# An AdaLN block with linear attention and top-2 experts: another order of the transfers on SyncE, and other orders on TensorE, VectorE and ScalarE

## The reference

```python
h = layernorm(x) * (1 + ca) + sa
x = x + ga * attn(h)          # 16 heads of 16; q, k = elu(.) + 1; causal linear attention:
                              # num = tril(q k^T) v + q S;  den = sum(q * cumsum(k));  out = num / den
h = layernorm(x) * (1 + cb) + sb
# experts: logits = h @ emb^T, top 2 of 8, softmax of the two, a token keeps a choice
# while its place among the expert's tokens (running count over all tokens) is <= 512
x = x + gb * sum_over_choices(weight * (relu(h @ W1[e]^T) @ W2[e]^T))
```

## Time and profile before

| what | us |
|---|---|
| median of three executions (lowest, highest) | 469.27 (468.74, 469.97) |
| the profiled execution, its own time | 468.47 |
| its span, first to last instruction | 466.7 |
| TensorE busy | 391.6 |
| VectorE busy | 334.7 |
| GpSimd busy | 225.4 |
| ScalarE busy | 204.7 |
| from the first scores of step 3 to those of the tail | 219.51 |

### The profile page before, as it was taken

How to read it: one execution, slowest core, us unless ns; L and a number is a source line. 1 busy time by engine, 2 the same in 40 slices (tenths; PEclk the granted TensorE clock), 3 DMA queues, 4 the chain that set the end, 5 groups by cost and what they waited for, 6 DMA issues and landing times.

```text
span 466.7 us, 9558 instructions
## 1 busy us (share of the span) xinstructions
PE 391.6 (84%) x3366; PEld 307.4 (66%) x3366; DVE 334.7 (72%) x876; ACT 204.7 (44%) x341; POOL 225.4 (48%) x231
## 2 busy tenths in 40 slices
PE   3696979999799899989989999896228999999981
PEld 0553748777577586767767778675107888888871
DVE  6573685999698698789879979867734656666640
ACT  1664335644545543554544572314105444444520
POOL 4223151553642480481473372442464788788454
PEclk9599899999899989989989999997558999999997
DMA  8102204006204404402510601546147688888343
GB/s 251 66 0 83 79 0 132 15 7 204 74 2 143 138 2 144 130 8 95 152 33 31 194 13 40 177 145 217 49 133 232 146 212 204 189 212 183 35 44 46
DMA packets 40340, 49.70 MB, mean 106 GB/s; under 512 B 5881, under 2 KB 32506, under 8 KB 40306
## 3 DMA queue, kind: packets, MB, share of 16 engines
q1 hardware_dynamic: 33138, 36.55, 24.8%
q0 software_dynamic: 7168, 12.72, 14.0%
HBM read 31.84 MB, written 17.42 MB: 106 GB/s over the span
## 4 chain that ended last, share of the span: by engine, by line
PE 39%; DVE 20%; issue 16%; POOL 8%; DMA 8%; ACT 4%; SPq 3%; POOLq 1%; DVEq 0%; ACTq 0%
DVE sT L1554 6%; PE bank L1345 4%; PE quad L1345 3%; PE bank L1347 3%; PE bank L1346 3%; PE quad L1347 3%; PE quad L1346 3%; PE quad L1085 3%; PE bank L1010 2%; PE bank L1117 2%; DMA rden_rows<-rden_flat 2%; DMA out<-x 2%; PE bank L1145 2%; DVE kcum L1520 2%; SPq L443 2%
## 5 line engine op out<-in xcount | busy, mean ns | idle before, releaser
L1554 DVE TENSOR_TENSOR sT<-quad,causal 128x1024 f32<-128x1024 f32 x64 | 74.6, 1206 | 1.6 <-PE quad L1085 1.6
L685 POOL DMA_INDIRECT out<-x,tok_i x32 | 52.6, 1643 | 25.2 <-DVE x L1859 18.5
L595 POOL TENSOR_TENSOR x<-x_sb,bo_g 128x1024 f32<-128x1024 f32 x8 | 18.9, 2363 | 76.2 <-DMA out<-x 76.0
L1085 PE MATMUL quad<-q_bd,kT 32*128 32x256 f32 x512 | 42.7, 403 | 6.9 <-DVE sT L1554 5.4
L1145 PE MATMUL bank<-wog,oT 128*128 128x256 f32 x128 | 36.2, 407 | 10.3 <-DVE oT L1544 10.3
L1345 PE MATMUL bank<-w_hi,in_hi 128*128 128x256 f32 x128 | 37.0, 289 | 6.2 <-DVE in_lo L1844 6.2
L674 POOL DMA_INDIRECT xg<-token_rows,tok_i x32 | 32.9, 1027 | 19.0 <-issue 9.1
L924 ACT ACTIVATE in_hi<-quad 128x512 fp32r<-128x512 f32 x32 | 19.1, 598 | 51.2 <-PE quad L1347 51.2
L1117 PE MATMUL bank<-sT,v_pad 128*32 128x128 f32 x1024 | 41.4, 281 | 0.0
L1844 DVE SCALAR_TENSOR_TENSOR in_lo<-quad,in_hi 128x512 fp32r<-128x512 f32 x32 | 22.1, 692 | 22.8 <-ACT in_hi L924 22.8
L1085 PEld LDWEIGHTS quad<-q_bd,kT 32*128 32x128 f32 x512 | 26.8, 184 | 15.3 <-DVE sT L1554 8.1
(11 more groups left out here) (219 smaller groups left out, 1016.9 us busy)
## 6 DMA issues: line engine op xcount, KB each, us to landing
token_rows<-h SPq DMA_DIRECT2D x8, 528.0 KB, 3.6
x_sb<-x SPq DMA_DIRECT2D x8, 512.0 KB, 3.7
token_rows<-mod_all SPq DMA_DIRECT2D x8, 512.0 KB, 4.8
out<-x SPq DMA_DIRECT2D x8, 512.0 KB, 5.1
w_sb<-w1T SPq DMA_DIRECT2D x8, 512.0 KB, 4.5
w_sb<-w2T SPq DMA_DIRECT2D x8, 512.0 KB, 4.7
rden<-rden_rows SPq DMA_DIRECT2D x56, 64.0 KB, 2.3
mod_all<-mod_rows SPq DMA_DIRECT2D x8, 384.0 KB, 4.1
```

The source lines that it names most:

```text
L685: gp.indirect_dma_start(out=out_rows, out_offset=bass.IndirectOffsetOnAxis(ap=tok_i[:, 1, at:at + 1], axis=0), in_=y_sb[q][:, t, :], in_of ...
L1085: last = mm(quad[:, r, k * 2 * P:(k + 1) * 2 * P].rearrange("p (s i) -> p s i", s=2), kT[b.p][at, k, tok(t)], q_bd[b.p][at, k, :, tok(t)], ...
L1554: v.tensor_tensor(sT[t % 2][:, 8 * a:8 * (a + 1), :].rearrange("p (r s) i -> p r (s i)", s=2), quad[:, 2 * a:2 * a + 2, :].rearrange("p r ...
```

## The change

- SyncE: in a full step the order becomes `rden_to_dram(attend)`, `load_ga(front)`, `load_x(early)`, `rden_to_heads(attend)`, `den_to_dram(front)`, `den_by_rows(front)`, `load_mod(attend)`, `x1_to_out(route)`, and then the wait for `row_on`, `rows_h` and `rows_gate`.
- GpSimd: `row_h(route)` goes from behind `norm2` to the end of the step, behind `norm1` and `q_times_kcum`.
- TensorE: `front_h` of half 0 comes first, before `scores(attend, 0)`, and half 1 behind `update_state(attend, 0)`; q of half 1 and k of half 0 stay in a row, but ahead of `numerator(attend, 0)`; the two transposes of `route_h` are in a row; logits come before `scores(attend, 3)`; the k transposes come before the v projections, which are in a row.
- VectorE: `low_h` right behind `mask(attend, 0)`; `early_stats` before `normalise(attend, 0)`; `k_sum` of half 1 first; `residual(attend, 1)` behind `route_top`; `mask(attend, 3)` behind `route_choose`; `keep_state(attend, 2)` later; `route_weights` behind `route_places`.
- ScalarE: h of half 0 first; denominators before the k and v copies; `normalise_x(early)` before the last v copy.
- The PSUM banks and TensorE's waits are set to suit.

The diff (context cut):

```diff
@@ -283,12 +283,12 @@
-        FH_ORDER, Q_ORDER, K_ORDER, SUM_ORDER = (1, 0), (1, 0), (0, 1), (0, 1)
+        FH_ORDER, Q_ORDER, K_ORDER, SUM_ORDER = (0, 1), (1, 0), (0, 1), (1, 0)
         V_ORDER, KT_ORDER, RH_ORDER = (0, 1), (0, 1), (0, 1)
-        H_BANK, Q_BANK, K_BANK = (ring[1], ring[0]), (ring[1], ring[0]), (ring[1], ring[0])
-        V_BANK, KT_BANK, RH_BANK = (ring[1], ring[1]), (ring[0], ring[0]), (ring[0], ring[1])
-        DEN_BANK, LOGIT_BANK, COUNT_BANK, LIST_BANK = ring[0], ring[1], ring[0], ring[1]
-        H1_ORDER, HI_ORDER, LO_ORDER = (1, 0), (1, 0), (1, 0)
+        H_BANK, Q_BANK, K_BANK = (ring[0], ring[1]), (ring[1], ring[0]), (ring[1], ring[0])
+        V_BANK, KT_BANK, RH_BANK = (ring[1], ring[0]), (ring[1], ring[1]), (ring[0], ring[1])
+        DEN_BANK, LOGIT_BANK, COUNT_BANK, LIST_BANK = ring[0], ring[0], ring[0], ring[1]
+        H1_ORDER, HI_ORDER, LO_ORDER = (0, 1), (0, 1), (0, 1)
         MOD_BANK = (bank[4], bank[6], bank[7])
@@ -465,23 +465,24 @@
                     return
+                if attend:
+                    rden_to_dram(attend)
+                if front:
+                    load_ga(front)
                 if early:
                     load_x(early)
-                if front:
-                    load_ga(front)
-                if attend:
-                    rden_to_dram(attend)
-                    load_mod(attend)
+                if attend:
                     rden_to_heads(attend)
...
                     den_to_dram(front)
+                    den_by_rows(front)
+                if attend:
+                    load_mod(attend)
                 if route:
+                    x1_to_out(route)
                     sp.wait_ge(S["row_on"], 2 * (route.n + 1))
...
                     rows_gate(route)
-                    x1_to_out(route)
-                if front and not is_last(front):
-                    den_by_rows(front)
@@ -637,11 +638,12 @@
                     norm2(route)
-                    row_h(route, xhat)
                 if early:
...
                     q_times_kcum(front)
+                if route:
+                    row_h(route, xhat)
@@ -813,11 +815,11 @@
                 act.wait_ge(S["h_mm"], KH * b.n + 1)
+                high_h(b, 0)
+                front_h(b, 0)
+                act.wait_ge(S["h_mm"], KH * b.n + 2)
                 front_h(b, 1)
                 high_h(b, 1)
-                act.wait_ge(S["h_mm"], KH * b.n + 2)
-                high_h(b, 0)
-                front_h(b, 0)
                 for i in range(KH):
@@ -835,11 +837,11 @@
                     act.wait_ge(S["h_mm"], KH * front.n + 1)
+                    high_h(front, 0)
+                    front_h(front, 0)
+                    act.wait_ge(S["h_mm"], KH * front.n + 2)
                     front_h(front, 1)
                     high_h(front, 1)
-                    act.wait_ge(S["h_mm"], KH * front.n + 2)
-                    high_h(front, 0)
-                    front_h(front, 0)
                     exp_q(front, 1)
@@ -852,17 +854,18 @@
                     spread_q(front)
-                    front_kt(front, 0)
                 if route:
...
                 if front:
+                    front_kt(front, 0)
+                    front_kt(front, 1)
                     front_v(front, 0)
-                    front_v(front, 1)
-                    front_kt(front, 1)
                 if early:
                     normalise_x(early)
+                if front:
+                    front_v(front, 1)
                 if is_last(front):
@@ -986,8 +989,8 @@
                 modulate(2)
+                front_v(b, 1)
                 wait(pe, S["v_on"], 2)
-                front_v(b, 1)
                 front_kt(b, 0)
@@ -1208,21 +1211,21 @@
                     pe.wait_ge(S["k_tok_on"], 2)
+                if front:
+                    wait(pe, S["v_on"], 4 * front.n)
+                    front_h(front, 0)
                 if attend:
                     scores(attend, 0)
+                    update_state(attend, 0)
                 if front:
-                    wait(pe, S["k_tok_on"], 2 * front.n)
-                    front_h(front, 1)
                     if route:
                         wait(pe, S["lists_on"], route.n)
-                    wait(pe, S["v_on"], 4 * front.n)
-                    front_h(front, 0)
+                    wait(pe, S["v_on"], 4 * (front.n - 1) + 2)
+                    front_h(front, 1)
                 if route:
...
                 if attend:
-                    update_state(attend, 0)
                     scores(attend, 1)
-                    numerator(attend, 0)
                 if front:
@@ -1231,12 +1234,13 @@
                 if attend:
+                    update_state(attend, 1)
+                    numerator(attend, 0)
                     scores(attend, 2)
...
                 if attend:
-                    update_state(attend, 1)
                     out_project(attend, 0)
@@ -1246,36 +1250,35 @@
                     route_h(route, 0)
-                if attend:
-                    update_state(attend, 2)
-                if route:
                     pe.wait_ge(S["q_on"], KH * front.n + 2)
...
                     out_project(attend, 1)
+                if route:
+                    pe.wait_ge(S["h2T_on"], KH * route.n + 1)
+                    route_logits(route)
+                if attend:
+                    update_state(attend, 2)
+                    scores(attend, 3)
                 if front:
                     if route:
-                        pe.wait_ge(S["h2T_on"], KH * route.n + 1)
+                        pe.wait_ge(S["h2T_on"], KH * route.n + 2)
+                    else:
+                        pe.wait_ge(S["q_on"], KH * front.n + 2)
+                    front_kt(front, 0)
+                    if route:
+                        pe.wait_ge(S["logits_on"], route.n + 1)
                     else:
                         pe.wait_ge(S["k_on"], KH * front.n + 2)
-                    front_kt(front, 0)
-                if route:
-                    pe.wait_ge(S["h2T_on"], KH * route.n + 2)
-                    route_logits(route)
-                if attend:
-                    scores(attend, 3)
-                    numerator(attend, 2)
-                if front:
-                    pe.wait_ge(S["k_tok_on"], 2 * front.n + 1)
                     if is_last(front):
...
                         front_den(front)
-                    if route:
-                        pe.wait_ge(S["logits_on"], route.n + 1)
-                    else:
-                        pe.wait_ge(S["q_on"], KH * front.n + 2)
-                    front_v(front, 0)
+                if attend:
+                    numerator(attend, 2)
+                if front:
+                    pe.wait_ge(S["k_tok_on"], 2 * front.n + 1)
+                    front_kt(front, 1)
                 if route:
@@ -1285,8 +1288,8 @@
                 if front:
-                    pe.wait_ge(S["v_on"], 4 * front.n + 2)
-                    front_v(front, 1)
+                    pe.wait_ge(S["k_tok_on"], 2 * front.n + 2)
+                    front_v(front, 0)
                     if route:
@@ -1294,11 +1297,11 @@
                             pe.wait_ge(S["den_on"], front.n + 1)
-                    front_kt(front, 1)
+                    front_v(front, 1)
                 if attend:
...
                 if route:
-                    pe.wait_ge(S["v_on"], 4 * front.n + 4)
+                    pe.wait_ge(S["v_on"], 4 * front.n + 2)
                     route_lists(route)
@@ -1717,63 +1720,64 @@
                     mask(attend, 0)
+                if front:
+                    low_h(front, 0)
+                    low_h(front, 1)
                 if route:
                     residual(route, 3)
-                if front:
-                    low_h(front, 1)
-                    low_h(front, 0)
-                if attend:
-                    mask(attend, 1)
+                if attend:
                     keep_state(attend, 0)
...
                     mean2(route)
+                if attend:
+                    mask(attend, 1)
                 if front:
                     q_max(front, 1)
-                    k_max(front, 0)
-                if attend:
-                    normalise(attend, 0)
                 if early:
...
                 if attend:
+                    normalise(attend, 0)
+                if front:
+                    k_max(front, 0)
+                if attend:
+                    keep_state(attend, 1)
                     residual(attend, 0)
                 if front:
-                    k_sum(front, 0)
                     k_max(front, 1)
-                if attend:
-                    keep_state(attend, 1)
-                if front:
+                    k_sum(front, 1)
                     q_max(front, 0)
...
                 if front:
-                    k_sum(front, 1)
+                    k_sum(front, 0)
                 if attend:
```

(11 more changed lines are left out.)

## The result

The changed kernel takes 485.27 us (median of 4 runs, 483.35 to 489.81) where the kernel before, beside it, takes 469.0 us: ratio 1.0356, 95% interval 1.0303 to 1.0408. It is slower, as forecast, but by 16.3 us instead of 8.2, and outside the range (451 to 484). The profiled execution took 486.62 us, its span 484.9. In all that follows medians are of all executions of a run, while ratios leave out those over 1.5% above the fastest of their kernel, which matters for two runs: the rest have a median of 467.5 instead of 470.6 us in sync_and_rowh, and of 466.3 instead of 467.7 in mask3_and_invert.

What follows compares the result with a forecast made beforehand. No single engine was taken to bound it: TensorE and VectorE nearly full, plus a 3.5 us stall a step through the queues. Work 31.1, standing and short waits made 38.0 us a step, +8.2 in all: 477.5 us, range 451 to 484.

Steps and rivals of the forecast that it cites:

- What it takes away: Out leaves mid-step, denominators no longer stand behind `load_x`: GpSimd's wait under 8 us, `normalise(attend, 0)` waits 0.3 us.
- Standing: VectorE held until a GpSimd elementwise instruction ends: `k_sum` 1.0, routing 2.4, `low_h` 0.3, x1 sum 2.2 us a step.
- routing: VectorE's `gap` 0.4, `one_hot` 1.4 and chained instructions 0.6 us behind GpSimd's `row_h` and bo_g: 2.4 us, bounds 0 and 3.
- the x1 sum: GpSimd's sum in `x_and_bias` meets VectorE's `route_places`, which stands 2.2 us, bounds 0 and 2.3; in step 8 `route_choose`.
- the four terms: VectorE's standing per step: `k_sum` 1.0, routing 2.4, `low_h` 0.3 and the x1 sum 2.2 us.
- Two signs: Marks of VectorE standing in routing, steps 3 to 8: `gap` lasting over 0.4 us and `one_hot` over 1 us.
- X: The end of VectorE's second scan, `k_sum(front, 0)`, from which the step's later times were counted; x1 sum at X + 14.2.
- VectorE's floor of 31.1 us: VectorE's own work in a step: busy 31.8 us without the 0.7 us that the first scan stood.
- short waits 1.0: VectorE's waits per step: scores at the start 0.6, denominators 0.3, q's exponential 0.1 us.
- The sum: Steps of 38.0 us, step 3 37.7: steps 3 to 8 take 227.7 against 219.5 us, +8.2.
- rival 2: Routing stands, but out lands outside `route_places` in steps 3 to 7: 466.8 us; chance 0.14.
- Rival 1: No standing in routing, the waits removed decide: steps of 33.5 us, 451 us; chance 0.28.

Runs made afterwards that it cites:

- sync_and_rowh: The kernel before with SyncE's new order and `row_h` moved to the end of GpSimd's step, other engines' orders kept: 470.6 us, ratio 0.993.
- mask3_and_invert: The changed kernel with `mask(attend, 3)` back ahead of `route_choose` and step 8's `invert_by_token` ahead of `normalise(attend, 2)`: 467.7 us, ratio 0.994.

## Why the prediction was right or wrong

1. **What it takes away**: right in the main. GpSimd waits 7.6 to 9.6 us for out instead of 10.3 to 13.5; the sign was under 8, which only step 6 kept. `normalise(attend, 0)` has no wait in steps 5 to 7 (in step 5 `early_stats` ahead of it waits 1.09 us for x), but 1.87 us in step 4 and 3.17 in step 8, where 0.3 was put down. SyncE's order alone is worth 6 us.

2. **Standing**: right in its sum. `k_sum` stands 1.06 us, 0.60 in step 4 (1.0), routing 0.20 + 1.58 + 0.49 = 2.3 us (2.4), `low_h` 0.6 to 0.9 (0.3), the x1 sum 1.9 to 2.2 us in each of steps 4 to 7 (2.2), and 0 in step 3 where it started at 111.85, after places and weights. Steps 4 to 7 have a mean standing of 6.07 us; the four terms made 5.9. In detail it was less good. Two signs failed: `gap` takes 0.34 us (over 0.4 was said) and `one_hot` 0.71 (over 1), because the cast `top_f` ahead of it, which the forecast let pass, stood for 1.58. And there was luck in the x1 sum. It starts 14.4 us after X in step 6 (14.2 forecast), but 15.8 to 16.4 after X in steps 3, 4, 5 and 7. VectorE was late as well, so they met all the same: at `in_slot` in step 5, at `in_list` in step 6, and only at `route_weights` (L1647), behind places, in steps 4 and 7. One-input instructions on bfloat16 stood as well (`in_list` at L1683 2.30 instead of 0.29 us, eight `in_slot` 3.54 instead of 1.39 in step 5). By the rule of the Trainium skill that the forecast quoted (SBUF — State Buffer, Who interferes with whom) they had to, and the trace agrees; the rows of before alone had left it open.

3. **VectorE's floor of 31.1 us**: 1.1 too high (own work is 30.0 us in steps 4 to 7 of the changed kernel). I took 0.64 us of scan out of 31.8 us of work; but 0.64 is step 6's, whose busy time in the profile is 30.73, and in the other steps of before the standing is 1.5 to 1.8 us. Own work is 29.6 to 30.5 in steps 3 to 7 of every kernel.

4. **The step that failed: "short waits 1.0".** Measured in steps 4 to 7 are 5.42, 2.70, 4.18 and 1.97 us, mean 3.57; in step 8 7.7. The least in any step of any run is 1.78: even where nothing is late there are some 0.8 to 1.4 us of gaps under 0.25 us between instructions, and 0.6 to 0.9 at the first scores. This alone is 1 us in each step, and it could be read before the change: step 3 lasts 34.10 us with VectorE busy for 31.95. The rest is the cover that I took for granted: TensorE's idle stretch and lower clock were said to be hidden, since VectorE is the late one. In steps 4, 6 and 8 they came back as VectorE's waits. As a cost in the kernel's time this is not shown, though: with the clock held up by filler in steps 4 and 6 these two lost 2.5 and 2.0 us of waits, steps 3 and 7 grew by 2.1 and 1.0 us, and step 8 was not reached. The waits term failed without the new orders too: for waits removed and no standing beyond the scan the forecast had steps of 33.5 us with 1.4 of waits, and with SyncE's order alone steps 4 to 7 take 36.1 us with 3.4 of idle time.

5. **The sum.** Steps 4 to 7: 158.65 us against 152, +6.65 (4 x 2.57 for idle and 4 x 0.17 for standing, less 4 x 1.08 for work). Step 3: 36.29 against 37.7, -1.4. Step 8: 42.2 against 38.0, +4.2. Together 237.2 against 227.7. Step 8 was costed by "as long" and "instead", without following its chain: its x1 sum holds up `route_choose` as forecast, and behind that `mask`, `normalise(2)` and `invert_by_token` come 3.7 us late for TensorE, whose queue then has to run at the lower clock.

6. **What it could not see**: that the two large standing terms hang on one place. They were costed as separate items, at 2.4 and 2.2 us, with rival 2 (466.8 us) for the second alone. The run with `mask(attend, 3)` back shows that what VectorE has in front of GpSimd's product decides both in steps 4 to 7. Rival 1 (451 us, no standing in routing) was too low for the same reason as point 4, and because the new orders then wait on TensorE; the best version found, SyncE's order alone, takes 463.

What stays open: which part of the new orders on the three engines costs the 9 to 11 us that remain once `row_h` is early (moving one numerator only moved the wait), and why step 2 took 1 to 7 us more in some executions of kernels with the new orders (step 3 began at 75.3 to 83.0 us). `normalise(attend, 3)` waits 3.8 us for TensorE there in all of them, long or not (2.8 with the old orders); in the three longest it is `normalise(attend, 2)` that waits 4.9 to 5.1 us instead of 2.5.

## What to carry to other kernels

Where VectorE and GpSimd both work in SBUF, cost an order by what stands on VectorE while a long GpSimd instruction runs: here a mask from PSUM was free (2.34 us beside the product, as alone), an 8-element cast cost the whole instruction, and the delay can push VectorE into the next meeting. A sum of busy times is no step time: add the idle time that the best step of the trace shows. And a queue's order is worth what it is only with its partners: SyncE's alone gave 6 us, the three engines' alone cost 37, through one small instruction that SyncE waits for and that had moved behind a long chain; and one piece put back undid the loss.

## What the runs showed of the hardware

A cast from uint32 to f32 over 8 elements a partition, one input, stood for GpSimd's whole product (0.14 us alone, 1.72 beside it), and so did a multiplication and comparisons on bfloat16 with one input. The clock of TensorE also fell without idle time worth the name just ahead: in the changed kernel's step 4 it was at 0.50 from 139 to 141 us, though TensorE had no idle stretch over 0.47 us since 128 (logits, a state update and scores run there, then transposes and `front_den`), and in the run with `row_h` back, in the stretch below, 4 us after an idle time of 1.5 us.

```profile
208.00:213.00 5.00, 5.00 (x28) 2.49 (x28) 4.64 (x28) 0.25 (x2) 0.98 (x2) 0.66 0.00 0
```
